# A fused FFN–attention–FFN kernel on one core: work moved between engines and units at the stage seams

## The reference

```python
x = x + 0.5 * ffn(layernorm(x))
x = x + attention(layernorm(x))        # 16 heads of 64, rotary + Fourier terms on q and k
x = x + 0.5 * ffn(layernorm(x))

# ffn: two shared experts and eight routed ones, all of them computed for every token
scores = softmax(x @ gate_w.T); topk_w, topk_idx = top_k(scores, 2)
topk_w = topk_w / (topk_w.sum(-1) + 1e-20)
pos = cumsum(one_hot(topk_idx)) - 1; keep = pos < capacity
comb = scatter(topk_w * keep)
y = einsum(silu(x @ we_gate) * (x @ we_up) @ we_down, comb) + shared
```

## Time and profile before

| | |
|---|---|
| median of 3 runs | 1273.29 us (1272.16 to 1274.07) |
| the profiled execution, its own time | 1275.4 us |
| its span in the trace | 1273.6 us |
| busy share of the span | PE 97%, DVE 75%, POOL 70%, ACT 49% |
| chain that ended last | PE 86%, issue 4%, POOL 4%, DVE 3%, DMA 1%, ACT 1% |
| granted PE clock, mean | 0.995 of full; 39 of the page's 40 slices at nine tenths or more |
| stages | first FFN to about 236 us, attention to about 1062 us, second FFN to the end |

### The profile page before, as it was taken

The page is one execution under the profiler, slowest core; times in us unless marked ns, Lnnn a source line. Parts: engine busy times, 40 slices in busy tenths (PEclk is TensorE's granted clock), DMA queues, the critical chain, the costliest instruction groups (busy, mean ns, idle before and its releaser), DMA issues.

```text
span 1273.6 us, 20947 instructions
## 1 busy us (share of the span) xinstructions
PE 1229.2 (97%) x7346; PEld 780.9 (61%) x7346; DVE 955.6 (75%) x1443; ACT 627.9 (49%) x917; POOL 896.2 (70%) x652
## 2 busy tenths in 40 slices
PE   4999999899999999999999999999999987999998
PEld 3666666556666566666666666666666644666665
DVE  6656777778888888888888888888787865656632
ACT  3444522455555546455556555555555552443422
POOL 0443346788998898898898899889889932543353
PEclk9999999999999999999999999999999998999999
DMA  5353150132333333232323232323232310443150
GB/s 169 134 183 91 43 150 17 33 66 54 70 58 67 61 64 64 63 65 59 69 60 68 60 68 60 68 57 70 51 77 52 76 19 19 141 142 108 43 158 17
DMA packets 118677, 95.35 MB, mean 75 GB/s; under 512 B 75760, under 2 KB 85008, under 8 KB 118320
## 3 DMA queue, kind: packets, MB, share of 16 engines
q1 hardware_dynamic: 118064, 93.75, 30.2%
q10 hardware_dynamic: 512, 0.26, 0.1%
HBM read 57.53 MB, written 2.88 MB: 47 GB/s over the span
## 4 chain that ended last, share of the span: by engine, by line
PE 86%; issue 4%; POOL 4%; DVE 3%; DMA 1%; ACT 1%; SPq 0%; POOLq 0%; DVEq 0%; ACTq 0%
PE banks L1156 16%; PE banks L453 15%; PE banks L1135 13%; PE banks L466 10%; PE banks L1074 6%; PE banks L994 5%; PE banks L1172 5%; PE banks L1140 4%; PE banks L1181 4%; PE banks L1002 3%; POOL work L1428 2%; PE banks L1113 1%; POOL turn L1418 1%; PE banks L415 1%; PE banks L408 1%
## 5 line engine op out<-in xcount | busy, mean ns | idle before, releaser
L1006 DVE TENSOR_REDUCE neg_max<-banks 128x2 f32<-128x1024 f32 x256 | 305.1, 1226 | 11.0 <-PE banks L994 6.2
L1256 ACT ACTIVATE work<-banks 128x1024 f32<-128x1024 f32 x256 | 262.4, 1026 | 93.8 <-PE banks L1140 77.6
L1156 PE MATMUL banks<-work 128*64 128x512 f32 x1024 | 233.8, 598 | 2.0 <-ACT work L1256 1.1
L1428 POOL TENSOR_TENSOR work<-work 128x1024 f32<-128x1024 f32 x64 | 159.6, 2494 | 81.4 <-PE banks L1156 81.3
L1418 POOL TENSOR_TENSOR turn<-turn,side_turned 128x512 f32<-128x512 f32 x128 | 163.7, 1301 | 29.8 <-DMA side_turned<-side 29.6
L1412 POOL TENSOR_TENSOR turn<-turn,fenc 128x512 f32<-128x512 f32 x128 | 162.8, 1291 | 2.0 <-DVE side L1327 2.0
L1423 POOL TENSOR_TENSOR qk_l<-turn,qk_h 128x512 fp32r<-128x512 f32 x128 | 161.8, 1285 | 2.8 <-ACT qk_h L983 2.8
L1156 PEld LDWEIGHTS banks<-work 128*64 128x64 f32 x1024 | 68.0, 136 | 135.0 <-issue 109.9
L1348 DVE TENSOR_TENSOR work<-work 128x1024 f32<-128x1024 f32 x64 | 105.4, 1647 | 38.2 <-PE banks L1156 38.2
L807 POOL TENSOR_TENSOR o_raw<-o_raw,work 128x512 f32<-128x512 f32 x52 | 66.9, 1289 | 89.8 <-DVE o_raw L723 89.7
L807 POOL TENSOR_TENSOR work<-work 128x512 f32<-128x512 f32 x44 | 56.5, 1292 | 96.7 <-DVE work L723 51.7
(11 more groups left out here) (177 smaller groups left out, 2459.3 us busy)
## 6 DMA issues: line engine op xcount, KB each, us to landing
work<-share SPq DMA_DIRECT2D x32, 1024.0 KB, 9.4
side_turned<-side SPq DMA_DIRECT2D x256, 128.0 KB, 3.1
rec_all<-rec_d SPq DMA_DIRECT2D x128, 128.0 KB, 3.0
x_tok<-in_x SPq DMA_DIRECT2D x8, 256.0 KB, 6.5
out<-x_tok SPq DMA_DIRECT2D x8, 256.0 KB, 9.4
work<-in_w_gate_up SPq DMA_DIRECT2D x1, 1280.0 KB, 7.2
work<-in_w_qk SPq DMA_DIRECT2D x1, 1024.0 KB, 9.7
den_d<-den_rows ACTq DMA_DIRECT2D x64, 4.0 KB
```

Of the source, the lines that this page charges most:

```text
L1006: return nc.vector.tensor_reduce(neg_max[:, g % 2, qt::DH], of, AX.X, ALU.max, negate=True)
L1156: ins = nc.tensor.matmul(o_bank(g)[OWN[h], :], v_all[:, kt, n * DH:(n + 1) * DH], pt[:, g % 2, kt, h * T:(h + 1) * T], start=(kt == 0), st ...
L1256: nc.scalar.activation(pt[:, g % 2, kt, :], S[kt].rearrange("p h q -> p (h q)"), ACT.Exp, scale=QSCALE).then_inc(s["probs"], 1)
L1428: nc.gpsimd.tensor_tensor(pt[:, g % 2, 2, :], pt[:, g % 2, 2, :], pt[:, g % 2, 3, :], ALU.add).then_inc(s["second_sum"], 1)
```

## The change

What it does, part by part:

- **Tokens.** The second FFN's normalised tokens of batch 1 are written by ACT right behind those of batch 0 (`odd_tokens`), no longer by DVE.
- **Last two pairs.** Pair 61's output uses bank 4 too (`own_bank(g)` is `g < N - 2`), so `apply_v(61)` waits for three of pair 63's four maxima. The fronts come behind `project_out` in period 62, with a wait for the copy of the output. In period 63 the logits come behind `apply_v(62)`; the denominators of pair 62 come behind the last two scores, then the turn of the logits, then `apply_v(63)`. On ACT `copy_den(62)` comes behind the last exponentials. On DVE the routing of the first chunk is cut in three (`ROUTE_PARTS`): steps 0 to 6, `first_sum(63)`, steps 7 to 17, `reciprocals(62)`, steps 18 to 21.
- **Tail.** `denominators(63)` and `copy_den(63)` go from unit 0 to unit 1, `reciprocals(63)` from unit 3 to unit 4, `reciprocals(62)` out of unit 1 (above).
- **Shares and positions one unit later**: in both FFNs and for all chunks, with the first chunk's routing steps 22 and 23. The middle routing steps of the later chunks are spread over one unit more.
- **Early norm.** The attention's norm of batch 0 is done in units 55 to 59 of the first FFN.

```diff
-LOGITS_AT, EXPS_AT, POSITIONS_AT, SHARES_AT = 8, 10, 14, 16
+LOGITS_AT, EXPS_AT, POSITIONS_AT, SHARES_AT = 8, 10, 15, 17
-ROUTE_AT = {9: range(0, 4), 10: range(4, 8), 11: range(8, 13), 12: range(13, 19), 13: range(19, 22), 14: range(22, 23), 15: range(23, 24)}
-FIRST_ROUTE_AT = {0: range(4, 12), 1: range(12, 19), 2: range(19, 22), 3: range(22, 24)}
+ROUTE_AT = {9: range(0, 4), 10: range(4, 7), 11: range(7, 10), 12: range(10, 13), 13: range(13, 16), 14: range(16, 20),
+            15: range(20, 22), 16: range(22, 24)}
+FIRST_ROUTE_AT = {0: range(4, 12), 1: range(12, 19), 2: range(19, 22), 4: range(22, 24)}
+ROUTE_PARTS = {"logits": range(0, 7), "experts": range(7, 18), "masks": range(18, 22)}
...
-            first_positions, first_shares = (1, 2) if last else (3, 4)
-            first_route = {1: range(22, 24)} if last else FIRST_ROUTE_AT
+            first_positions, first_shares = (2, 3) if last else (4, 5)
+            first_route = {2: range(22, 24)} if last else FIRST_ROUTE_AT
...
+                def odd_tokens():
+                    act.wait_ge(s["normed"], 1)
+                    for t in range(TT):
+                        n = TT + t
+                        ins = nc.scalar.activation(xn2[1][:, t, :], x_tok[:, 1, t, :], ACT.Identity,
+                                                   scale=rs_c[:, n:n + 1], bias=shift_c[:, n:n + 1])
+                    ins.then_inc(s["xn_first"], 1)
...
                 if ahead == "tokens":
                     tokens(0)
+                    odd_tokens()
...
-                elif ahead == "tokens":
-                    first_tokens()
...
-                elif ahead == "route":
-                    for n in range(22):
+                elif ahead in ROUTE_PARTS:
+                    for n in ROUTE_PARTS[ahead]:
                         route(n, 0)
...
-            EARLY_NORM_AT = {-14: range(0, 4), -13: range(4, 7), -12: range(7, 10), -11: range(10, 13), -10: range(13, 16)}
+            EARLY_NORM_AT = {-15: range(0, 4), -14: range(4, 7), -13: range(7, 10), -12: range(10, 13), -11: range(13, 16)}
...
             def own_bank(g):
-                return g < N - 3
+                return g < N - 2
...
                         if own_bank(g):
-                            pe.wait_ge(s["maxes"], (g + 2) * TT + 3)
+                            pe.wait_ge(s["maxes"], min((g + 2) * TT + 3, N * TT))
...
# PE, period(p)
-                    if p == JOIN_LOGITS_AT:
-                        ffn2["tensor"](pe, "logits")
                     if exists(last):
                         for kt in range(TT):
                             apply_v(last, kt)
-                    if p == JOIN_LOGITS_AT:
-                        ffn2["tensor"](pe, "turn")
                     if exists(nxt):
                         turn_maxima(nxt, p)
-                    if p == JOIN_FRONTS_AT:
-                        ffn2["tensor"](pe, "fronts")
+                    if p == JOIN_LOGITS_AT:
+                        ffn2["tensor"](pe, "logits")
...
                     if exists(p - 3):
                         project_out(p - 3, p)
-                    if exists(last):
+                    if p == JOIN_FRONTS_AT:
+                        pe.wait_ge(s["o_copied"], p)
+                        ffn2["tensor"](pe, "fronts")
+                    if exists(last) and p != JOIN_LOGITS_AT:
                         denominators(last, p)
...
                     scores(N - 1, 2)
                     scores(N - 1, 3)
+                    denominators(N - 2, N - 1)
+                    ffn2["tensor"](pe, "turn")
                     for kt in range(TT):
                         apply_v(N - 1, kt)
                 elif tail == 0:
                     project_out(N - 3, N)
+                elif tail == 1:
                     denominators(N - 1, N)
...
# ACT: copy_o(last) now ahead of ffn2's "logits" in period 63; then
-                    copy_den(N - 2)
                     exponentials(N - 1, 2)
                     exponentials(N - 1, 3)
+                    copy_den(N - 2)
                     ffn2["scalar"](act, "exps")
                     copy_o(N - 1)
-                elif tail == 0:
+                elif tail == 1:
                     copy_den(N - 1)
...
# DVE
-                    if p == JOIN_TOKENS_AT:
-                        ffn2["vector"](dve, "tokens")
...
-                    if p == JOIN_LOGITS_AT:
-                        ffn2["vector"](dve, "route")
...
                     for p in PERIODS:
                         period(p)
+                    ffn2["vector"](dve, "logits")
                     first_sum(N - 1)
+                    ffn2["vector"](dve, "experts")
+                    reciprocals(N - 2)
+                    ffn2["vector"](dve, "masks")
                 elif tail == 1:
-                    reciprocals(N - 2)
                     residual(N - 3)
-                elif tail == 3:
+                elif tail == 4:
                     reciprocals(N - 1)
```

More of the change, by code:

```diff
@@ L1294, in period @@
                         high(act, ahead, Q)
+                    if exists(last):
+                        copy_o(last)
                     if p == JOIN_LOGITS_AT:
                         ffn2["scalar"](act, "logits")
-                    if exists(last):
-                        copy_o(last)
                     if p == JOIN_TOKENS_AT:
```

## The result

The changed kernel took 1265.84 us (median of 5 runs, 1264.72 to 1266.66) against 1273.29 for the one before (5 runs, 1272.16 to 1274.07): a ratio of 0.9941, 95% interval 0.9927 to 0.9956. That is 7.45 us less; 13.5 were forecast, and the range ended at 1265.0. The direction was right, the size was not. The profiled executions differ by more, 9.6 us of span (1273.6 to 1264.0), and part of the miss lies in that difference.

A forecast was written before the change was run, and what follows sets the result against it. PE, busy 97% of the span, was taken to set the time. Seam 10.8, early norm 1.9 and start 0.8 summed to 13.5 us, taken off the median 1273.29: 1259.8, range 1256.5 to 1265.0.

The forecast's parts named there:

- part 9: Later chunks' positions, shares and routing: 0, the shares' DMA starting 2.2 us later under enough cover.
- part 4: Seam, first sum of pair 63 ahead of the expert steps: -3.8 us from apply_v(63) to the first down projection.
- part 5: Second FFN's start, reciprocals of pair 62 early: PE's wait for normalise(62) and low clock behind it mostly go, -3.4 us.
- part 8: First FFN's start: the 2.1 us mask wait and half clock go, new waits come for gated(2) and shares, -0.8 us.
- 2 and 3: Last attention periods: apply_v(61) in bank 4, -0.8 us, and the new order of period 63, -2.1 us.
- part 6: Second FFN's unit 11: the share chain comes late, a new wait of 1.0 us and 0.3 for the second expert, +1.3.
- 7: Early norm a unit sooner: PE's 1.9 us wait in unit 61 for its last step goes, -1.9 us.
- A: Rival, chance 0.2: the clock falls behind two of the new waits, about 1.7 us each come back, 1262.5 us.
- B: Rival, chance 0.15: DVE's expert steps pass POOL's sum unhindered, waits in units 2 and 11 shrink together by 2 us, 1257.8.
- C: Rival, chance 0.12: only the waits move, a longer share chain returns the seam's saving at unit 11; with 4 more, 1263.8.
- D: Rival, chance 0.03: slower, through a share chain starting much later; reciprocals of pair 63 written at 1090 would give 1277.
- E: Rival, chance 0.04: gains hidden, the seam's idle passes to the next stall, first wait and early norm do not pay; within 0.2%.

The follow-up runs named there:

- r2: The changed kernel with routing steps 0 to 21 of the later chunks in their old units, positions and shares still one unit later: 1260.24 us.
- r3: The kernel before, with only the later chunks' routing spread and positions and shares one unit later: 1276.31 us.
- r1: The changed kernel with positions, shares and routing steps of the later chunks back in their old units: 1262.92 us.
- r4: The kernel before, with only the change's parts at the seam of attention and second FFN: 1262.85 us.
- r9: The kernel of r2 with the first sum of pair 63 behind all routing steps again: 1264.69 us.
- r10: The kernel of r2 with the reciprocals of pair 62 back in unit 1: 1262.38 us.
- r7: The kernel of r2 with the reciprocals of pair 63 back in unit 3: 1259.62 us.
- r5: The kernel of r2 with the attention's early norm back in units 56 to 60: 1263.2 us.
- r12: The changed kernel itself, timed again on the chip of the follow-up runs: 1264.56 us.
- r11: The kernel of r7 with the first FFN's first shares in unit 6 and no wait there for the copied shares: 1260.73 us.

## Why the prediction was wrong

**The step that failed is part 9.** "Positions, shares and routing of the later chunks: 0" was costed from the shares' transfer alone, and that cover was real: the shares came in time in every chunk, and r2 shows that the shift is free. The part looked at what moved one unit and not at what moved two. The mask step went from unit 14 to unit 16 of the window, its user from 16 to 17; PE waited for it in each of six chunks. The ledger puts the bill at 3.8 us (0.4, 0.6, 1.4 in the first FFN, 0.5, 0.4, 0.4 in the second), r3 at 3.6, and r1 against the change at 2.9 (2.3 against each one's own before); the waits for the masks are 2.3 of it and the one for `comb_w` 0.5. With the spread alone undone (r2) the kernel took 1260.24, half a microsecond above the forecast of 1259.8.

**A second error, argued and not tested by a run, is in the sum's last step.** The profiled execution of before stood 2.1 us above the median, and I took the whole sum off the median. But some 6 us of the sum were low clock (2.8 in part 4, some 1.7 in part 5, up to 1.5 in part 8), and the low clock is not the same in every run of before: its mean granted clock was 0.995 in the profiled execution, 0.993 to 1.0 in 41 other runs, 0.997 in 22 of them. The profiled one had more of it than most, so more could be won there than in the median. r4, whose expectation took about 2 us off for this, came out as expected (1262 to 1264; 1262.85). With 13.5 less 3.8 less 2.1 the sum is 7.6, against 7.45. That it fits so closely is luck: without the spread r1 is 9.8 below its before and r2 12.4, so the two leave between 1 and 4 us of the 13.5 to this second error.

By parts:

- 1 (tokens, -2.0): right in the trace (2.3 by the ledger); alone it was worth 4.15.
- 2 and 3 (to `apply_v(63)`, -4.9 together with 1): 4.94 sooner. The profiled attention ran 0.5 late there, so 5.5.
- 4 (first sum, -3.8): from `apply_v(63)` to the first down projection 12.9 us, forecast 13.4. The new wait in unit 2 was 0.83, not 1.5. Undone (r9), it costs 4.4 or 3.4 (the second against each one's own before), with half clock in two stretches of the profiled execution.
- 5 (reciprocals of pair 62): no wait left in unit 5; undone (r10), it costs 1.0 to 2.1 in the medians and 0.4 in the trace, where most of it is given back at unit 11. Of the forecast 3.4, some 1.7 were low clock.
- 6 (shares, +1.3): a wait of 1.35 in unit 11, as said, and moving `reciprocals(63)` to unit 4 is its cause (r7). DVE gave them at 1072.23 and POOL's first product began at 1085.61 (forecast 1072.2 and 1085.9).
- 7 (early norm, -1.9): the units 60 to 62 took 1.9 less. But unit 60 was by then 2.1 late by the spread, so the two cancel in the ledger (+0.26 at unit 62). The step was to end 0.4 us before PE asks; it ended 0.7 after, and the wait stayed at that. From r2 (r5), the move is worth 1.9 to 3.0 in the medians and 2.0 in the trace.
- 8 (start, -0.8): -0.3. The two waits are there (1.0 for the product, 1.2 for `comb_w`), and a third that I had missed: 0.45 of the first down projection of batch 1 for the copied shares.

Rivals: A did not happen in the first profiled execution (clock 1.00 in all three windows), but it did, once, in that of r12, behind the share wait of 1.72 us: so it happens to this kernel in some executions. Its price of 1.7 us for a stretch is near the 1.4 to 1.5 that the ledgers of r12 and r10 show. B did not: a two-input step was held for 2.37 us. By the Trainium skill, "SBUF — State Buffer", section "Who interferes with whom", the step with one tensor input passes and the one with two blocks, and whoever issues first is the one that goes on. The trace agrees: the two-input step L696 at 1056.77, already running when POOL began at 1056.93, took its 0.22, and the next one was held; the one-input maximum L694 took 0.21 in each of the seven places where POOL was at work, and the two-input L696 behind it 0.64 to 0.70 in place of 0.22. C, D and E did not happen: a wait of 1.35 came back at unit 11, as part 6 said. The seam, where nearly all the working went, gave 11.5 against 10.8; the loss came from the part that got two sentences.

What stays open: why the tokens alone also spare the low clock behind a wait of 2.56 us, why r2's median is 2.7 below r1's when the traces differ by 0.7, and how many executions of each kernel have low clock where: each has one profile (the change two), and the medians cannot say.

## What to carry to other kernels

When producer and consumer are both moved in a hand-written schedule, count the distance between them before and after, for every pair, in the units of the engine that lags: here a producer whose engine lags by a unit or two had 0.5 to 2.4 us of cover at a distance of two units (a unit is 2.23 us), and none at one. Compare two traces of the same work by a ledger of one repeated instruction; the list of waits named the masks too, as one row of 2.3 us in all, but the ledger said where the time went and what it cost together with what follows, 3.8. And where part of a profiled execution ran at a low clock, look at how often the other runs did before booking that as a gain.

## What the runs showed that was not expected

The granted clock's mean differed from run to run of one kernel (before: 0.993 to 1.0, 1269.5 to 1276.7 us over 41 runs), and the kernels with shorter waits had less low clock (r11: 1.0, 1.0, 1.0, 0.999, within 1 us), though not always less spread (r7: 1259.26 to 1262.86 at 0.999 to 1.0). Nor does half clock need a wait of about 2 us ahead of it, as each of the three stretches of the earlier trace rows had: in r10 it came at 35.0 behind waits of 1.25, 1.22 and 0.45 us, and in the same place, behind waits of 1.17, 1.23 and 0.45, it did not come in r12. And a step of 0.22 us on DVE took 1.35 beside work of POOL that DVE itself had released 0.2 us before: with POOL waiting for DVE's product in each unit, the two-input steps written behind that product are the ones that are held.
